# Attention followed by a two-band convolution: the output banks leave PSUM already divided by their row sums

## The reference

```
attn = softmax(q.T @ k * scale)                  # 4096 x 4096 for each image
x1   = gamma * (Wo @ (v @ attn.T)) + x
low  = mean of 2x2 in 8x8 patches; high = p - up2(low)
out  = up2(prelu(bn(mag_w @ low + b))) + prelu(bn(phase_w @ [high, roll(high)] + b))[:C]
```

## Time and profile before

| | |
|---|---|
| median of 3 runs | 2341.44 us (2340.3 to 2342.3) |
| profiled execution | 2340.45 us, span 2338.5 us |
| TensorE matmuls busy | 2205.9 us, 94% |
| VectorE busy | 1782.4 us, 76% |
| ScalarE busy | 1431.6 us, 61% |
| GpSimd busy | 677.7 us, 29% |
| granted TensorE clock, mean | 0.984 |

### The profile page before, as it was taken

One profiled execution on the slowest core, in us unless ns is written; L12 is line 12 of the kernel. 1 busy time (PEld: TensorE's weight loads), 2 busy tenths in 40 slices (PEclk: granted clock), 3 DMA queues, 4 the chain that ended last, 5 costly groups with the idle time before them and its releaser, 6 DMA issues.

```text
span 2338.5 us, 48099 instructions
## 1 busy us (share of the span) xinstructions
PE 2205.9 (94%) x16373; PEld 1764.1 (75%) x16373; DVE 1782.4 (76%) x3388; ACT 1431.6 (61%) x2547; POOL 677.7 (29%) x891
## 2 busy tenths in 40 slices
PE   5799999999989999999998999999999999999997
PEld 4577777777767777777777777777777777777776
DVE  6777877777867788877786877777877777778764
ACT  3457666657656666666656666566665656666663
POOL 3232332232322323322232321323322232233321
PEclk8799999999999999999999999999999999999998
DMA  4254444454554444444474443443445444344443
GB/s 159 59 115 94 99 109 102 84 117 99 135 131 85 110 107 92 109 108 97 93 168 102 99 99 72 104 96 91 103 111 133 75 89 93 77 82 88 84 86 64
DMA packets 596617, 235.02 MB, mean 101 GB/s; under 512 B 547072, under 2 KB 548352, under 8 KB 596576
## 3 DMA queue, kind: packets, MB, share of 16 engines
q1 hardware_dynamic: 596576, 234.51, 45.5%
HBM read 67.67 MB, written 32.53 MB: 43 GB/s over the span
## 4 chain that ended last, share of the span: by engine, by line
PE 64%; DVE 15%; issue 10%; DMA 5%; ACT 3%; POOL 1%; SPq 1%; DVEq 0%; ACTq 0%; POOLq 0%
PE M L482 13%; PE M L519 7%; PE O L631 7%; PE O L633 6%; PE O L632 6%; PE O L644 6%; PE O L646 6%; PE O L645 6%; DVE pq L1052 5%; DMA pt<-pq 4%; PE S L590 4%; DVE saved L947 4%; DVE pmax L943 2%; DVE pl L1047 2%; PE M L500 1%
## 5 line engine op out<-in xcount | busy, mean ns | idle before, releaser
L758 ACT ACTIVATE ph<-S 128x512 f16<-128x512 f32 x512 | 307.6, 601 | 525.5 <-PE S L590 524.8
L644 PE MATMUL O<-uh,pt 128*128 128x257 f16 x2048 | 568.2, 277 | 16.9 <-DMA pt<-pq 16.7
L631 PE MATMUL O<-uh,ph 128*128 128x257 f16 x2048 | 570.3, 278 | 4.5 <-DVE pl L1047 4.1
L633 PE MATMUL O<-uh,pl 128*128 128x257 f16 x2048 | 563.2, 275 | 0.0
L632 PE MATMUL O<-ul,ph 128*128 128x256 f16 x2048 | 561.8, 274 | 0.0
L646 PE MATMUL O<-uh,pt 128*128 128x257 f16 x2048 | 559.0, 273 | 0.0
L645 PE MATMUL O<-ul,pt 128*128 128x256 f16 x2048 | 555.7, 271 | 0.0
L947 DVE TENSOR_SCALAR_CACHE_REDUCE saved<-M 128x512 f32<-128x512 f32 x512 | 344.0, 687 | 257.0 <-PE M L519 253.0
L1047 DVE TENSOR_TENSOR pl<-p,ph 128x512 f16<-128x512 f32 x512 | 402.6, 787 | 60.5 <-ACT p L761 59.1
L519 PE MATMUL M<-kst,qst 96*128 (+1 forms) x1024 | 424.0, 442 | 20.9 <-DVE saved L947 16.2
L1052 DVE TENSOR_TENSOR pq<-saved,pq 128x512 f16<-128x512 f32 x512 | 387.6, 757 | 19.2 <-ACT saved L770 19.1
(11 more groups left out here) (161 smaller groups left out, 2907.4 us busy)
## 6 DMA issues: line engine op xcount, KB each, us to landing
xr<-in_x SPq DMA_DIRECT2D x53, 512.0 KB, 3.8
out_y<-z SPq DMA_DIRECT2D x33, 512.0 KB, 3.0
xb<-in_x SPq DMA_DIRECT2D x25, 512.0 KB, 3.7
pt<-pq SPq DMA_TRANSPOSE x512, 3.1
qraw<-q_scratch SPq DMA_DIRECT2D x99, 64.0 KB, 2.0
uh_scratch<-uh_next SPq DMA_DIRECT2D x24, 257.0 KB, 3.2
uh<-uh_scratch SPq DMA_DIRECT2D x24, 257.0 KB, 3.2
ul_scratch<-ul_next SPq DMA_DIRECT2D x24, 256.0 KB, 3.1
```

Source lines behind the costliest of these rows:

```text
L631: nc.tensor.matmul(O[j][:, 0:UW], ph[:, i % 4, q], uh[:, i, :], start=(i == 0), stop=False)
L633: ins = nc.tensor.matmul(O[j][:, 0:UW], pl[:, i % 4, q], uh[:, i, :], start=False, stop=False)
L644: nc.tensor.matmul(O[j][:, 0:UW], pt[:, k % RING, i, :], uh[:, t, :], start=False, stop=False)
```

## The change

oraw shrinks from 257 to 256 columns a bank. The four O banks become one PSUM tensor, so that one instruction can read column 256 of all four. VectorE's new find_gains waits for the last slot of the turn, takes the four reciprocals straight from PSUM and multiplies by ogain. Copies on both engines wait for that result (rs_step) in place of their own bank's slot, and write the bank multiplied by its gain: ScalarE by an activation whose scale is a column of rs, VectorE by a multiplication by a column of rs. normalise and its semaphore on_ready go; the y tasks wait for both copies' semaphores. In the FULL turns find_gains stands at the head of VectorE's turn, in the others behind the first pl.

```diff
--- before.py
+++ after.py
@@ -173,7 +173,7 @@
         nbias = sb("nbias", [128, SUB])
         p32 = sb("p32", [128, 2, CH])
         ph, pl = sb("ph", [128, 4, CH], f16), sb("pl", [128, 4, CH], f16)
-        oraw = sb("oraw", [128, SUB, UW])
+        oraw = sb("oraw", [128, SUB, C])
         rs = sb("rs", [128, SUB])
         y = sb("y", [128, CT, ROWS, WID])
         low = sb("low", [128, CT, LOWN])
@@ -200,7 +200,8 @@
 
         odd_hi, odd_lo = [buf[:, :, 1:ROWS + 1, :].rearrange("p t r w -> p t (r w)") for buf in (hh, hl)]
 
-        O = [ctx.enter_context(nc.psum_tensor(f"O{i}", [128, 512], f32)) for i in range(SUB)]
+        O_all = ctx.enter_context(nc.psum_tensor("O", [128, SUB, 512], f32))
+        O = [O_all[:, j, :] for j in range(SUB)]
         S = [ctx.enter_context(nc.psum_tensor(f"S{i}", [128, 512], f32)) for i in range(2)]
         M = [ctx.enter_context(nc.psum_tensor(f"M{i}", [128, 512], f32)) for i in range(2)]
 
@@ -230,7 +231,7 @@
         pe_started = sem("pe_started")
         u_stored = sem("u_stored")
         u_direct_loaded, u_turned_loaded = sem("u_direct_loaded"), sem("u_turned_loaded")
-        o02_out, o13_out, rs_step, on_ready = sem("o02_out"), sem("o13_out"), sem("rs_step"), sem("on_ready")
+        o02_out, o13_out, rs_step = sem("o02_out"), sem("o13_out"), sem("rs_step")
         pairs_ready, low_ready, high_ready = sem("pairs_ready"), sem("low_ready"), sem("high_ready")
         hh_ready, conv_in = sem("hh_ready"), sem("conv_in")
         zneg_ready = sem("zneg_ready")
@@ -599,7 +600,8 @@
                         pe.wait_ge(x_split[0], EVEN_FIRST + g)
                         ins = project_kq(bank, (xbh, xbl)) if kind == "kq" else project_u(bank, (xbh, xbl), task[1])
                     elif kind == "y":
-                        pe.wait_ge(on_ready, g + 2)
+                        pe.wait_ge(o02_out, 2 * g + 2)
+                        pe.wait_ge(o13_out, 2 * g + 2)
                         ins = transposed(bank, task[1])
                     elif kind == "low":
                         pe.wait_ge(conv_in, g + 1)
@@ -681,7 +683,8 @@
             for n, task in TAIL.numbered[0]:
                 pe.wait_ge(m_free[n % 2], use(TAIL, ALL, n))
                 if task[0] == "y":
-                    pe.wait_ge(on_ready, ALL + 2)
+                    pe.wait_ge(o02_out, 2 * ALL + 2)
+                    pe.wait_ge(o13_out, 2 * ALL + 2)
                     ins = transposed(M[n % 2], task[1])
                 elif task[0] == "low":
                     pe.wait_ge(conv_in, ALL + 1)
@@ -747,9 +750,9 @@
 
             def copy_out(g, j):
 
-                act.wait_ge(k_weighed, NK * g + RING - SUB + j + 1)
+                act.wait_ge(rs_step, 2 * g + 2)
                 act.wait_ge(high_ready, g + 1)
-                nc.scalar.activation(oraw[:, j, :], O[j][:, 0:UW], ACT.Copy).then_inc(o02_out, 1)
+                nc.scalar.activation(oraw[:, j, :], O[j][:, 0:C], ACT.Copy, scale=rs[:, j:j + 1]).then_inc(o02_out, 1)
 
             def probabilities(g, i):
                 act.wait_ge(s_filled, ND * g + i + 1)
@@ -866,7 +869,7 @@
 
 
 
-            nc.vector.memset(half[:, :, :], -0.5).then_inc(on_ready, 1)
+            nc.vector.memset(half[:, :, :], -0.5)
             nc.vector.memset(quarter[:, :], 0.25).then_inc(out_stored, 16)
             nc.vector.memset(uh[:, :, C:C + 1], 1.0).then_inc(qsave_free, 16)
             nc.vector.memset(uh_next[:, :, C:C + 1], 1.0).then_inc(u_stored, 32)
@@ -1025,22 +1028,19 @@
             finish_q(M[n % 2], 1, m_free[n % 2])
             dve.wait_ge(scanned, NCH)
 
+            def find_gains(g):
+
+                dve.wait_ge(k_weighed, NK * g + RING)
+                dve.wait_ge(o02_out, 2 * g)
+                nc.vector.reciprocal(rs[:, :], O_all[:, :, C]).then_inc(rs_step, 1)
+                dve.wait_ge(rs_step, 2 * g + 1)
+                gain = ogain[:, ds((g + (ALL - 1)) % ALL // NCH, 1)]
+                nc.vector.tensor_tensor(rs[:, :], rs[:, :], gain.to_broadcast([128, SUB]), ALU.mult).then_inc(rs_step, 1)
+
             def copy_out(g, j):
 
-                dve.wait_ge(k_weighed, NK * g + RING - SUB + j + 1)
-                nc.vector.tensor_copy(oraw[:, j, :], O[j][:, 0:UW]).then_inc(o13_out, 1)
-
-            def normalise(g):
-                dve.wait_ge(o02_out, 2 * g + 2)
-                dve.wait_ge(o13_out, 2 * g + 2)
-                nc.vector.reciprocal(rs[:, :], oraw[:, :, C]).then_inc(rs_step, 1)
-                dve.wait_ge(rs_step, 2 * g + 1)
-                gain = ogain[:, B - 1:B] if isinstance(g, int) else ogain[:, ds((g + (ALL - 1)) % ALL // NCH, 1)]
-                nc.vector.tensor_tensor(rs[:, :], rs[:, :], gain.to_broadcast([128, SUB]), ALU.mult).then_inc(rs_step, 1)
                 dve.wait_ge(rs_step, 2 * g + 2)
-                for j in range(SUB):
-                    ins = nc.vector.tensor_scalar(oraw[:, j, 0:C], oraw[:, j, 0:C], rs[:, j:j + 1], None, ALU.mult)
-                ins.then_inc(on_ready, 1)
+                nc.vector.tensor_scalar(oraw[:, j, :], O[j][:, 0:C], rs[:, j:j + 1], None, ALU.mult).then_inc(o13_out, 1)
 
             def low_probabilities(g, i):
                 dve.wait_ge(probs_ready, ND * g + i + 1)
@@ -1102,6 +1102,7 @@
             def turn(g, parity, c, plan, scans):
                 if plan is not FULL:
                     low_probabilities(g, 0)
+                find_gains(g)
                 copy_out(g, 1)
                 copy_out(g, 3)
                 if plan is FULL:
@@ -1111,8 +1112,6 @@
                         finish_chunk(g)
                     if t + 1 < MT and UNITS[t + 1][0] == "d":
                         low_probabilities(g, UNITS[t + 1][1])
-                    if t == (0 if plan is FULL else 1):
-                        normalise(g)
                     if t == 1 and plan is not FINAL:
                         low_q(g + 2)
                     if t == SCAN and scans:
@@ -1137,9 +1136,9 @@
                 find_scale(image + 1, 1 - parity)
 
             turns(dve, turn, before_image)
+            find_gains(ALL)
             copy_out(ALL, 1)
             copy_out(ALL, 3)
-            normalise(ALL)
             for n, task in TAIL.numbered[0][:CT]:
                 dve.wait_ge(m_filled[n % 2], use(TAIL, ALL, n) + 1)
                 add_residual(M[n % 2], ALL, task[1], m_free[n % 2])
```

## The result

The changed kernel takes 2365.29 us (median of 5 runs, 2362.61 to 2368.14) against 2340.30 us of the kernel before (2338.26 to 2342.30): a ratio of 1.0107, 95% interval 1.0093 to 1.0122. It is 25.0 us slower; 30.6 were forecast.

A forecast was written before the change was run, and what follows sets the result against it. TensorE was taken as the bound, with VectorE mostly waiting for it. FULL turns 18.5, image starts 1.9, LAST and FINAL turns 11.0, less 0.8 at the end, made 30.6 us slower: 2372 us, range 2352 to 2383.

The forecast's parts named there:

- The seam of a FULL turn: Between turns, late gains delay ScalarE's exps, then its second u copy, VectorE and an M bank: 0.88 us in 21 turns, 18.5.
- One sign: In FULL turns, TensorE would idle 0.8 to 0.9 us ahead of the maximum scores in unit 5, released by VectorE's maximum.
- The step that was off: Later in a FULL turn VectorE waits for TensorE, so nothing pays back the 0.88 us lost.
- Image starts: Three turns that open an image, where TensorE already waits for ScalarE's first exp: 0.62 us each, 1.9 in all.
- LAST turns: Turns without opening projections, where tiles 0 and 1 come late: 1.37 us each, 11.0 over eight with FINAL.
- The end: Behind the last turn, TensorE's wait before the first transposition falls from 2.27 to 1.5 us: a gain of 0.8.
- Covered seams: Rival: unseen slack swallows the 0.88 us in FULL turns; only the other terms count, +12.1 us, 2353.5; chance 0.17.
- The late DMA of slot 0: Rival: the transposing DMA for slot 0 lands late, 0.5 us more in 21 turns, +41, 2382; chance 0.09.
- Faster by VectorE's backlog: Rival: 1.1 us less VectorE work a turn frees M banks earlier, -24 us, 2317; chance 0.08.

The follow-up runs named there:

- e5: The kernel before, with every copy waiting for the turn's last slot instead of its own bank's, and nothing else of the change: 2345.49 us.
- e1: The changed kernel with ScalarE's first exp pair ahead of its copy of bank 0 in FULL turns: 2350.96 us.
- e2: The changed kernel with ScalarE's second u copy ahead of the exps of tile 4 in FULL turns: 2358.80 us.
- e3: The changed kernel with ogain's column fixed at 0, so no index is computed: 2357.68 us.
- e4: The changed kernel with ScalarE's copies still waiting for the gains but not multiplying by them: 2357.78 us.
- e6: The kernel before without three and a bit of VectorE's four multiplications in place: 2335.24 us.
- e7: The changed kernel with the gains of banks 0 to 2 found after slot 14, bank 3's after slot 15; ScalarE's copies wait only for the first: 2336.80 us.

## Why the prediction was right, and where it was off

**The seam of a FULL turn.** Right in its steps up to ScalarE's exps, and in the delay that reaches the M bank. From the first scores: copy 0 at 1.03 forecast and 1.09 measured, the exp at 1.40 and 1.46, TensorE's fill of the M bank 0.88 later forecast and 1.00 measured. Two prices inside compensate: the reciprocal from PSUM is 0.18 and not 0.245, but it starts 0.37 after the scores where copy 3 started 0.28 after them, which I put down to the second wait ahead of it. A register operation of 45 ns of that wait's line (L1034) stands there in the trace; in e5, without that wait, VectorE's copies again start 0.28 after them. No run takes the second wait out by itself. e1 and e2 show the order on ScalarE and the path through the second u copy; e3 and e4 show the index and the scale as terms of 7.6 and 7.5 us.

One sign failed. The forecast wanted one idle of 0.8 to 0.9 ahead of the maximum scores; the record has 0.33 there. The delay comes in three parts, 0.28, 0.29 and 0.43. The first is TensorE waiting for ScalarE's exp at the scores of tile 4, a path that the forecast left out. The time of the M bank's fill came out near the forecast all the same, because the wait there only adds what is missing to 1.00; but the other path leaves 0.30 a turn in e2, where the one that was forecast is gone.

**The step that was off** is "Later in the turn VectorE again waits for TensorE, not the reverse, so nothing pays this back". The delay is 1.0 at slot 0 and 0.76 at the end of that turn; over 21 turns it is 0.66 each, 13.9 us and not 18.5. In the traces of this turn two of TensorE's later waits shrink: the one of 0.37 for the transposing DMA before slot 2 falls to 0.09, and takes the delay from 1.01 to 0.70; a wait for VectorE's saved maxima falls from 0.47 to 0.26. Between them a wait for a row maximum grows from 0.11 to 0.33. These three account for the 0.76 within 0.04. The whole run agrees in kind: TensorE waits 9.0 us less for the DMA and 6.5 less for the saved maxima. So the loss per turn is 0.66 because waits that TensorE already had later in the turn take up a third of the delay. No experiment isolates them.

**Image starts.** 1.9 forecast, 3.5 measured. The three turns are 81.4, 78.9 and 75.9 us long in the kernel before and 82.3, 78.6 and 78.8 in the changed one: +0.9, -0.3 and +2.9. In the second, TensorE's wait for ScalarE's exp grows from 5.78 to 6.38, just the 0.60 that was forecast (0.62), yet the turn is no longer. In the third the wait grows from 4.24 to 5.72, more than was forecast, and TensorE ran at a lower clock behind it. The rows of the waits, and the five us from the end of the third turn's wait on (us, busy us by engine, PE clock), the kernel before and then the changed one:

```profile
672.09 0.79 PE L590 MATMUL S<-qcur,kst 128*128 128x512 f32 x1 [5.78 <-ACT p L761]
...
1237.40:1242.40 5.00, 4.62 (x25) 3.17 (x26) 4.04 (x10) 4.95 (x12) 0.00 (x0) 0.66 0.06 13
```

```profile
677.77 0.80 PE L591 MATMUL S<-qcur,kst 128*128 128x512 f32 x1 [6.38 <-ACT p L764]
...
1248.65 0.80 PE L591 MATMUL S<-qcur,kst 128*128 128x512 f32 x1 [5.72 <-ACT p L764]
...
1248.60:1253.60 5.00, 4.68 (x19) 2.90 (x20) 3.66 (x6) 4.95 (x11) 0.00 (x0) 0.50 0.07 16
```

The granted clock in these five us was 0.66 before and 0.50 after. Over the nine traces this turn takes between 75.9 and 78.8 us, and 78.8 in e5, which has neither the late gains nor the scale. So much of its +2.9 may belong to the executions traced and not to the change. The delay of 0.6 is seen in the second turn; the sum of 3.5 stays open.

**LAST turns.** 1.37 forecast, 1.24 measured. The steps hold: tile 0 waits 1.32 instead of 0.28 and is 1.02 later from the first scores (1.08 forecast), tile 1 is 1.52 later (1.6). By tile 3 the delay is back to 1.02, so 0.5 are given back where 0.23 were forecast; in some of the seven turns a wait for the DMA adds 0.3 later. The near agreement of 1.24 with 1.37 is in part luck. Not seen in the forecast: without the late gains the saved multiplications would be worth 0.5 a turn here (e6, e7).

**The end.** 0.8 forecast. From the end of slot 15 to the end of the span it was 27.9 us before and is 26.0. The wait before the first transposition fell from 2.27 to 1.48, the 0.8 of the forecast:

```profile
2338.83 1.06 PE L501 MATMUL M<-ident,oraw 128*128 128x128 f32 x8 [1.48 <-DVE oraw L1043]
```

The eight transpositions took 1.88 before and 1.06 now. Granted clock of these two us (us, busy us by engine, PE clock), the kernel before, the changed one, and e5 with the row of its transpositions:

```profile
2312.80:2314.80 2.00, 1.88 (x8) 1.51 (x8) 0.74 (x2) 0.00 (x0) 0.00 (x0) 0.53 0.00 0
```

```profile
2338.80:2340.80 2.00, 1.06 (x8) 0.85 (x8) 1.29 (x2) 0.00 (x0) 0.00 (x0) 0.95 0.19 73
```

```profile
2317.93 1.06 PE L500 MATMUL M<-ident,oraw 128*128 128x128 f32 x8 [2.60 <-DVE oraw L1042]
...
2317.90:2319.90 2.00, 1.06 (x8) 0.86 (x8) 1.29 (x2) 0.00 (x0) 0.00 (x0) 0.90 0.00 0
```

In the kernel before they ran at 0.53 of the full 2.4 GHz, near the 1.2 GHz level, and in the changed one at 0.95. It is tempting to put this down to the shorter standing, 1.48 us instead of 2.27, but e5 stood 2.60 us and its transpositions took 1.06 at 0.90 all the same. Every trace but that of the kernel before has 1.06 or 1.07. So the 0.8 us of the clock are not shown to come from the change, and the end gained them by luck. The rest of the 1.9 us is later matmuls of the end (the run of eight that took 2.68 takes 2.20).

**The rivals.** Covered seams: no, the new waits stand in the FULL turns, 0.66 us each; but a later wait that shrinks, which this rival named, does take up a third of the delay. The late DMA of slot 0: no, slot 0 starts without a wait, 1.01 late like its neighbours. Faster by VectorE's backlog: wrong in sign for the whole, and by e6 worth 0.5 us in seven turns and nothing in the FULL ones.

## What to carry to other kernels

An instruction that reads all banks at once waits for the last of them, and so does everything that is queued behind its consumers in order: before merging small operations into one wide read, list what stands behind the consumer in its queue. The wait alone cost nothing in the FULL turns here (e5); the reciprocal, the index and the scale behind it did. Work taken off an engine pays only where that engine is the last to arrive; here that was in 7 of 32 turns and at the end, and the same idea came out 0.1% below the kernel before (2336.80 against 2339.52) once the gains of three banks no longer waited for the fourth. An address that needs registers costs its computation if it stands between two instructions on the path; to compute it ahead of the wait is the likely cure, which no run here tried.

## What the runs showed of the hardware

Reading four elements with a stride of a bank from PSUM, the reciprocal took 182 ns against 172 out of SBUF, 10 ns more; the forecast had taken 70 ns, from a copy of 257 elements out of PSUM (424) against a multiplication of 256 out of SBUF (351). VectorE's multiplication of 256 elements out of PSUM by a tile's column takes 480 ns where the plain copy of 257 took 424; the forecast had them equal. ScalarE's copy takes 478 ns with its scale read from a tile and 391 with a constant one (e4). A register computation of 174 ns between two VectorE instructions made the gap between them 0.26 us instead of 0.03 (e3). Eight transpositions ran at 0.53 of the clock after TensorE had stood for 2.27 us, at 0.95 after 1.48 us and at 0.90 after 2.60 us (one trace of each), so how long it stood did not by itself decide the clock.
